# Mixing stage of a two-block kernel: another order of the work on TensorE and ScalarE, and the two best experts by plain maxima

## The reference

```python
o = o * rsqrt(mean(o * o, axis=-1) + 1e-6) * rms_w      # per head, 16 heads of 8 channels
x = x + ga * (o.reshape(B, L, Dm) @ Wout.T + bout)      # attention output, gated
h = layernorm(x) * (1 + cb) + sb                        # per token, modulated per sequence
# experts: 8, of which each token takes 2
xn     = rms_norm(h, norm_scale)
scores = einsum('bsd,ed->bse', xn, w_router)
_, ids = top_k(scores, 2)
c      = take_along_axis(softmax(scores), ids)
y      = w_down[e] @ (val * silu(gate))                 # for the two experts of each token
x      = x + gb * (sum over the two of y * c, + h)
```

## Time and profile before

| what | value |
|---|---|
| median of three runs | 2890.2 us |
| the profiled execution's own time | 2890.03 us |
| its span | 2888.2 us |
| PE, PEld, DVE busy | 2127.3, 1794.5, 1984.2 us (74, 62, 69%) |
| ACT, POOL busy | 1274.1, 1390.6 us (44, 48%) |

### The profile page before, as it was taken

The page is one execution under the profiler, slowest core; times in us unless marked ns, Lnnn a source line. Parts: engine busy times, 40 slices in busy tenths (PEclk is TensorE's granted clock), DMA queues, the critical chain, the costliest instruction groups (busy, mean ns, idle before and its releaser), DMA issues. The chain is left out here.

```text
span 2888.2 us, 43460 instructions
## 1 busy us (share of the span) xinstructions
PE 2127.3 (74%) x12482; PEld 1794.5 (62%) x12482; DVE 1984.2 (69%) x6018; ACT 1274.1 (44%) x3003; POOL 1390.6 (48%) x1241
## 2 busy tenths in 40 slices
PE   4689888888988856645466646888886655199994
PEld 4578787777878733323245535777765654199993
DVE  6677777777777879972288877787885444255556
ACT  3534444343444411212266625667773432265551
POOL 2344444544444402137355555888884244544440
PEclk8799999999999967765577778999997665599996
DMA  3000000000000030013211000000003011122216
GB/s 92 15 1 1 1 1 1 1 1 1 1 1 1 1 131 27 19 51 42 63 56 44 30 0 1 1 1 1 1 1 129 20 34 35 45 69 66 65 54 177
DMA packets 103530, 92.63 MB, mean 32 GB/s; under 512 B 11840, under 2 KB 93888, under 8 KB 102592
## 3 DMA queue, kind: packets, MB, share of 16 engines
q1 hardware_dynamic: 80256, 63.36, 7.1%
q0 software_dynamic: 14592, 22.30, 3.0%
q10 hardware_dynamic: 8448, 4.20, 0.5%
HBM read 46.84 MB, written 42.98 MB: 31 GB/s over the span
## 5 line engine op out<-in xcount | busy, mean ns | idle before, releaser
L658 PEld LDWEIGHTS attn_out<-attn_turned,attn_v_diag 128*128 128x128 f32 x2048 | 300.1, 191 | 36.1 <-issue 26.2
L658 PE MATMUL attn_out<-attn_turned,attn_v_diag 128*128 128x256 f32 (+7 forms) x2048 | 304.7, 304 | 23.6 <-DVE attn_turned L828 23.6
L716 ACT ACTIVATE attn_p_att<-attn_score,attn_mx 128x224 f32<-128x224 f32 (+7 forms) x512 | 149.1, 391 | 385.3 <-DVE attn_mx L806 385.3
L2185 POOL TENSOR_TENSOR delta_A<-delta_A,delta_sW 128x256 f32<-128x256 f32 x256 | 186.2, 727 | 98.2 <-ACT delta_sW L2065 74.2
L2002 PE MATMUL delta_u<-delta_v_own,tables_sb 128*128 128x256 f32 x512 | 161.7, 399 | 77.4 <-ACT delta_v_own L2054 77.4
L647 PE MATMUL attn_score<-attn_k,attn_q_diag 128*128 128x256 f32 (+3 forms) x1024 | 211.7, 348 | 2.3 <-ACT attn_p_att L716 2.3
L2773 POOL DMA_INDIRECT choice_rows<-ffn_y,ffn_xg x136 | 130.3, 958 | 172.5 <-DVE ffn_y L2880 168.5
L2131 DVE TENSOR_TENSOR delta_u<-delta_u,xT 128x256 f32<-128x256 f32 x256 | 153.5, 600 | 83.6 <-PE delta_u L2006 77.1
L2065 ACT ACTIVATE delta_sW<-delta_W,tables_sb 128x256 f32<-128x256 f32 x256 | 128.7, 503 | 145.6 <-issue 122.0
L2194 POOL TENSOR_TENSOR delta_m<-delta_A,qT 128x1024 f32<-128x1024 f32 x64 | 183.8, 2872 | 5.0
L704 ACT ACTIVATE attn_p_geo<-attn_kp_wide,attn_geo_cols 128x32 f32<-128x32 f32 (+6 forms) x448 | 180.1, 518 | 0.0
(11 more groups left out here) (373 smaller groups left out, 5712.4 us busy)
## 6 DMA issues: line engine op xcount, KB each, us to landing
ffn_xg<-rows SPq DMA_DIRECT2D x136, 66.0 KB
acc<-route_zero SPq DMA_DIRECT2D x10, 832.0 KB
proj_rows<-acc SPq DMA_DIRECT2D x32, 256.0 KB, 4.2
comb_rows<-choice_rows SPq DMA_DIRECT2D x32, 256.0 KB
rows<-route_rows SPq DMA_DIRECT2D x16, 320.0 KB, 3.5
load_rows<-in_x SPq DMA_DIRECT2D x16, 256.0 KB
x_kept<-xT SPq DMA_DIRECT2D x16, 256.0 KB
out<-comb_done ACTq DMA_DIRECT2D x16, 256.0 KB
```

The source lines that it names most:

```text
L658: last = nc.tensor.matmul(O[kind][:, gr * T + SLOT * n:(gr + 1) * T], v_diag[:, gr * KB + n], turned[:, kind, gr, n * T + SLOT * n:(n + 1) ...
L716: last = nc.scalar.activation(p_att[:, gr, ROW_OFF[n]:ROW_OFF[n + 1]], score[at][:, c:c + SLOT * (n + 1)], ACT.Exp, bias=mx[:, gr, n:n + 1])
L2185: nc.gpsimd.tensor_tensor(A[:, t % 8], A[:, (t - 1) % 8], sW[:, t % 4], ALU.add).then_inc(k.A, 1)
```

## The change

On TensorE the functions `project_out` and `channels` take one half and alternate, project_out first; `back(b+1)` and `sum_rows(b)` come before `router_and_rows(b)`; `sum_heads` runs one chunk further ahead and stands last. The row sums move to the PSUM bank of the head sums, with a further wait in `sum_heads` for their reading. On ScalarE `add_bias` and `modulate` alternate by halves; `copy_rows` is split, its first half ahead of `add_bias`, its second behind `square`; `exps` comes behind it and waits for the mask. On VectorE `statistics` comes before `skip`, and `choose` is written anew: for each of the two choices the largest score by a reduction, an equality with it, a product with 8 - e (`from_end`), so that among equal scores the lowest index has the largest number, its maximum, and an equality with that as the one-hot row; before the second choice the first one's score is lowered by 3e38. The exponentials are now taken of all scores in their own order, with the two best appended (10 instead of 8 columns of a tile).

```diff
-    ROUTE = 2 * SIDE + 7
-    MASKED = 2 * SIDE + 4
+    ROUTE = 17
+    MASKED = 14
+    FAR = -3.0e38
...
-        seen = s.sb("seen", [128, 2])
-        top = s.sb("top", [128, SIDE, 8])
-        top_at = s.sb("top_at", [128, SIDE, 8], U32)
+        from_end = s.sb("from_end", [128, E1])
+        best = s.sb("best", [128, SIDE, K1])
+        tied = s.sb("tied", [128, SIDE, E1])
+        first = s.sb("first", [128, SIDE])
+        rest = s.sb("rest", [128, SIDE, E1])
         onehot = s.sb("onehot", [128, SIDE, K1, E1])
         mask = s.sb("mask", [128, SIDE + 1, E1], BF16)
-        less = s.sb("less", [128, SIDE, E1])
-        ex = s.sb("ex", [128, SIDE, E1])
+        less = s.sb("less", [128, SIDE, E1 + K1])
+        ex = s.sb("ex", [128, SIDE, E1 + K1])
...
-        head_sums, narrow_ps = sums[:, 0:128], sums[:, 128:256]
-        row_sums, logits, counts = small[:, 0:SIDE], small[:, 8:8 + SIDE * E1], small[:, 72:72 + (SIDE + 1) * E1]
+        head_sums, narrow_ps, row_sums = sums[:, 0:128], sums[:, 128:256], sums[:, 256:256 + SIDE]
+        logits, counts = small[:, 0:SIDE * E1], small[:, SIDE * E1:(2 * SIDE + 1) * E1]
...
-            pe.wait_ge(c.consts, 4)
+            pe.wait_ge(c.consts, 5)
 
             def sum_heads(i):
                 if i > 0:
                     pe.wait_ge(c.heads_read, i)
+                if i > 2:
+                    pe.wait_ge(c.sums_read, i - 2)
...
-                if 0 <= b <= LAST:
-                    channels(b)
-                if b + 1 <= LAST:
-                    project_out(b + 1)
+                if b == -1:
+                    sum_heads(1)
+                for par in both:
+                    if b + 1 <= LAST:
+                        project_out(b + 1, par)
+                    if 0 <= b <= LAST:
+                        channels(b, par)
                 if b >= 1:
                     count(b - 1)
-                if b + 2 <= LAST:
-                    sum_heads(b + 2)
-                if 0 <= b <= LAST:
-                    router_and_rows(b)
                 if b + 1 <= LAST:
                     back(b + 1)
                 if 0 <= b <= LAST:
                     sum_rows(b)
+                    router_and_rows(b)
+                if b + 3 <= LAST:
+                    sum_heads(b + 3)
...
+            def copy_rows(i, par):
+                if par == 0:
+                    act.wait_ge(c.newton, ROOT * (i + 3))
+                act.wait_ge(k[par].turned, i + 1)
+                if i > 1:
+                    act.wait_ge((k[par].sent0, k[par].sent1)[i % 2], 16 * TILES * K1 * (i // 2))
+                for r in range(TILES):
+                    j = par * TILES + r
+                    last = nc.scalar.activation(rows[:, i % 2, par, r, :, 0:D],
+                                                rowt[par][:, None, 128 * r:128 * r + 128].to_broadcast([128, K1, D]),
+                                                ACT.Copy, scale=root_y[:, i % 2, j:j + 1])
+                last.then_inc(k[par].rows_read, 1)
...
-                act.wait_ge(c.route, ROUTE * i + SIDE + 1)
+                act.wait_ge(c.route, ROUTE * i + MASKED)
                 nc.scalar.activation(ex[:, :, :], less[:, :, :], ACT.Exp).then_inc(c.exp, 1)
 
             def scale_up(n):
@@ -2494,17 +2496,21 @@
                     narrow(b + 1)
                 if 0 <= b <= LAST:
                     norm(b)
-                if b + 1 <= LAST:
-                    add_bias(b + 1)
+                if b >= 1:
+                    copy_rows(b - 1, 0)
+                for par in both:
+                    if b + 1 <= LAST:
+                        add_bias(b + 1, par)
+                    if 0 <= b <= LAST:
+                        modulate(b, par)
                 if 0 <= b <= LAST:
-                    modulate(b)
                     square(b)
                 if b >= 1:
+                    copy_rows(b - 1, 1)
                     exps(b - 1)
-                    copy_rows(b - 1)
                 if 0 <= b < PIECES:
                     scale_up(b)
-                if 2 <= b + 3 <= LAST:
+                if b + 3 <= LAST:
                     head_squares(b + 3)
...
+            nc.vector.tensor_scalar(from_end[:, :], g.t("iota")[:, 0:E1], -1.0, float(E1), ALU.mult, ALU.add).then_inc(c.consts, 1)
...
-                nc.vector.tensor_copy(seen[:, 0:1], score[:, 0, 0:1])
-                for j in range(SIDE):
-                    then(nc.vector.max(top[:, j, :], score[:, j, :]), wait=False)
-                then.done()
-                if i > 0:
-                    dve.wait_ge(c.exp, i)
-                then(nc.vector.tensor_tensor(less[:, :, :], top[:, :, :], top[:, :, 0:1].to_broadcast([128, SIDE, E1]), ALU.subtract),
-                     wait=False)
-                for j in range(SIDE):
-                    then(nc.vector.max_index(top_at[:, j, :], top[:, j, :], score[:, j, :]), wait=False)
-                then.done()
-                then(nc.vector.tensor_copy(g.chosen1[:, tiles(i), :], top_at[:, :, 0:K1]))
-                then(nc.vector.tensor_tensor(onehot[:, :, :, :], g.t("iota")[:, None, None, 0:E1].to_broadcast([128, SIDE, K1, E1]),
-                                             g.chosen1[:, tiles(i), :][:, :, :, None].to_broadcast([128, SIDE, K1, E1]), ALU.is_equal))
+
+                def first_best(scores, n):
+                    then(nc.vector.tensor_reduce(best[:, :, n], scores[:, :, :], AX.X, ALU.max))
+                    then(nc.vector.tensor_tensor(tied[:, :, :], scores[:, :, :], best[:, :, n:n + 1].to_broadcast([128, SIDE, E1]),
+                                                 ALU.is_equal))
+                    then(nc.vector.tensor_tensor(tied[:, :, :], tied[:, :, :], from_end[:, None, :].to_broadcast([128, SIDE, E1]),
+                                                 ALU.mult))
+                    if n == 0:
+                        if i > 0:
+                            dve.wait_ge(c.exp, i)
+                        then(nc.vector.tensor_tensor(less[:, :, 0:E1], scores[:, :, :], best[:, :, 0:1].to_broadcast([128, SIDE, E1]),
+                                                     ALU.subtract), wait=False)
+                    then(nc.vector.tensor_reduce(first[:, :], tied[:, :, :], AX.X, ALU.max))
+                    then(nc.vector.tensor_tensor(onehot[:, :, n, :], tied[:, :, :], first[:, :, None].to_broadcast([128, SIDE, E1]),
+                                                 ALU.is_equal))
+
+                first_best(score, 0)
+                then(nc.vector.scalar_tensor_tensor(rest[:, :, :], onehot[:, :, 0, :], FAR, score[:, :, :], ALU.mult, ALU.add))
+                first_best(rest, 1)
+                then(nc.vector.tensor_tensor(less[:, :, E1:E1 + K1], best[:, :, :], best[:, :, 0:1].to_broadcast([128, SIDE, K1]),
+                                             ALU.subtract), wait=False)
                 if i > 0:
                     dve.wait_ge(c.mask, i)
                 with nc.allow_low_precision(reason="sums of one-hot rows are 0 or 1"):
-                    then(nc.vector.tensor_reduce(mask[:, 0:SIDE, :], onehot[:, :, :, :].rearrange("p j c e -> p j e c"), AX.X, ALU.add),
-                         wait=False)
+                    then(nc.vector.tensor_tensor(mask[:, 0:SIDE, :], onehot[:, :, 0, :], onehot[:, :, 1, :], ALU.add), wait=False)
...
-                then(nc.vector.tensor_reduce(total[:, :], ex[:, :, :], AX.X, ALU.add))
+                then(nc.vector.tensor_reduce(total[:, :], ex[:, :, 0:E1], AX.X, ALU.add))
                 then(nc.vector.reciprocal(total[:, :], total[:, :]))
-                then(nc.vector.tensor_tensor(g.gate1[:, tiles(i), :], ex[:, :, 0:K1], total[:, :, None].to_broadcast([128, SIDE, K1]),
+                then(nc.vector.tensor_tensor(g.gate1[:, tiles(i), :], ex[:, :, E1:E1 + K1], total[:, :, None].to_broadcast([128, SIDE, K1]),
                                              ALU.mult))
...
+                if b + 1 <= LAST:
+                    statistics(b + 1)
                 if 0 <= b <= LAST:
                     skip(b)
-                if b + 1 <= LAST:
-                    statistics(b + 1)
...
-        g.chosen1, g.gate1 = (ctx.enter_context(nc.sbuf_tensor(n, tiles, F32)) for n in ("chosen1", "gate1"))
+        g.gate1 = ctx.enter_context(nc.sbuf_tensor("gate1", tiles, F32))
```

More of the change, by code:

```diff
@@ L2324, in widen, with project_out @@
                     last.then_inc(k[par].wide, 1)
-            def project_out(i):
-                for par in both:
-                    pe.wait_ge(k[par].on, i + 1)
-                    nc.tensor.matmul(mid[par][:, :], w_out[:, :], on[:, par, :], start=True, stop=True)\
-                        .then_inc(k[par].out_made, 1)
+            def project_out(i, par):
+                pe.wait_ge(k[par].on, i + 1)
+                nc.tensor.matmul(mid[par][:, :], w_out[:, :], on[:, par, :], start=True, stop=True).then_inc(k[par].out_made, 1)
             def back(i):
@@ L2340, in back, with channels @@
```

(28 more changed lines are left out.)

34 lines of the change are left out of this document (2 added, 32 removed).

## The result

| kernel | median of 5 runs | profiled span |
|---|---|---|
| before | 2890.2 us (2885.93 to 2891.28) | 2888.2 us |
| after | 2873.25 us (2868.9 to 2875.14) | 2873.4 us |

The ratio is 0.9944, with a 95% interval of 0.993 to 0.9959. The change gains 17 us where 57 were forecast; the time lies 3 us above the range.

A forecast was written before the change was run, and what follows sets the result against it. The VectorE, TensorE, ScalarE circle was taken as the bound, GpSimd idle a third of the time. Seven steps of 126.5 + 1.5 + 42 = 170 us against 228.2, with 0.9 for the first slot: -57, so 2833 us; range 2805 to 2870.

The forecast's parts named there:

- The bound and the loop's own path: Mixing stage: VectorE, TensorE, ScalarE circle sets the pace; new loop 21.0 to 21.5 us without unexplained waits, GpSimd's floor 21.0.
- rival 1: Mixing stage becomes GpSimd-bound with no late increments: seven steps of 21.3 us, -78 us, 2812 us; chance 0.22.
- The choice: VectorE, 15 chained instructions: 3.8 us against 3.1 for the old without its stall, the extra 0.7 us hidden in steady loops.
- stall B: VectorE's unexplained 3.2 us wait behind MAX8 in each loop, read as late semaphore increments; counted as gone in steady loops.
- makes GpSimd wait in full: Choice's two-SBUF-input instructions beside indirect DMAs: would add 1.8 us a group, up to 13 us in seven steps; not expected.
- The orders: Mixing loop: statistics right behind shares, then skip, roots not waiting for row sums, first indirect DMA within 1 us of its slots.
- The unexplained waits: Late increments beside indirect DMAs in the mixing loop: 4 us a loop taken, bounds nothing to 8.2 us.
- A: VectorE's unexplained wait of about 5 us before the roots, for row sums TensorE had already finished; read as late increments.
- rival 2: Late increments stay in full in the mixing loop: 29.3 us a loop, -33 us, 2857 us; chance 0.18.
- 128.0 forecast: The first five slot steps: 25.3 us each, with 1.5 us more in the first.
- the last two: Sixth and seventh slot steps: 21.0 us each, at GpSimd's own floor, 42 us together.
- The first slot: Start of the mixing stage: first slot 0.9 us later than 2263.93, for the dearer choice.

The follow-up runs named there:

- e_after_post: Kernel after with five row buffers instead of two, GpSimd sending nothing until five chunks are routed; 2914.9 us in its only run, 20.7 us a step without DMAs.
- e_choice: The new choice alone, in the orders of the kernel before; 2877.56 us, ratio 0.9957 to the kernel before.
- e_order: The new orders alone, with the MAX8 choice of the kernel before; 2872.39 us, ratio 0.9944 to the kernel before.
- the probe: Kernel after with small stages behind its end; 64 transposes beside 16 indirect DMAs seen 10.3 us late, 0.7 with three short memsets between the DMAs.
- e_half: Kernel after with the mixing stage's squares in bf16; 2802.47 us (0.9859) beside 2843.69 before, and again 2858.97 us (0.9881) beside 2891.64.

## Why the prediction was wrong, point by point

- **The bound and the loop's own path: right.** Worked out as 21.0 to 21.5 us; 20.7 without DMAs (`e_after_post`), and 21.1 beside them on kind N, where GpSimd is the bound. On that kind rival 1 is what happens: forecast steps of 21.3, measured 21.6 in the mean.
- **The choice: right in price, without effect.** 3.5 us for 3.8, in seven of eight chunks without gaps. But the reason given for that was wrong. The prediction held that stall B needs a burst of increments as MAX8 gives; `e_choice` has gaps of 2.8 to 5.1 us a chunk in the new choice, and `e_order` has lost the wait behind MAX8 with MAX8 still there. Nor did the price matter, since the chain of choices wasn't the path: with MAX8 left in, the time was the same on kind L (2872.39 and 2873.25) and, with bf16 squares, on kind N. The prediction weighed whether, by the Trainium skill (SBUF — State Buffer, Who interferes with whom), the new choice makes GpSimd wait in full. The trace doesn't show it: of the 27 indirect DMAs that overlap the choice in the kernel after, the longest took 1.01 us, for 0.96 in the median of all 128.
- **The orders: right in what they move.** Statistics behind the shares, roots without a wait, first DMA 1.2 us behind its slots. But the score behind the roots now waits 2.5 to 7.9 us in five chunks for TensorE's router sums ("remote"), which the prediction hadn't.
- **The unexplained waits: here it failed.** The prediction said that A "sits behind TensorE's longest stretch", that the sums now come well ahead of it, and left 4 us of late increments in a loop, with 8.2 as the upper end (rival 2). The lateness isn't tied to the row sums: as the runs have it, it meets what TensorE has finished while the group of DMAs is sent, and the new orders only moved it from the row sums, which the change took off the path, to `narrow`, which is on it. There it is 12.0 us, above the 8.2 that were taken as the upper bound because they were the whole of what stood in the old loop. A step on kind L is then 1.16 us from slots to first DMA, 20.23 for the group, 2.59 until `narrow` is seen, 7.80 until the next slots: 31.8 us; with the MAX8 choice (`e_order`) such steps are 31.8 to 33.0. In the five full loops that is 158.4 us against 128.0 forecast; in the last two 49.6 against 42.
- **The first slot**: 5.4 us later instead of 0.9. 2.9 us of that were there when the stage began (its first instruction starts at 2209.8 for 2206.9), and 2.5 us came in it. But from the stage's start to the first slot the kernel after takes 56.2 us in its other profile of kind L and 55.0 on kind N, where the result's has 59.5 and the kernel before 57.0; so that part isn't the change's steady price.
- Together the miss in steps and first slot is 38.0 + 4.5 = 42.5 us: -57 becomes -14.5, and the spans differ by -14.8.
- The forecast took the chip for given. On kind N the gain is 31 us. No profile of the kernel before was taken there. If the whole gain lies in the steps, its own are (151.4 + 31.4) / 7 = 26.1 us, an estimate, and the change removes 4.5 us from each. The nearest profiles on kind N, the kernel before with bf16 squares and with the memsets, have seven steps of 171.3 and 187.4 us together, on either side of that 182.8.

What is settled: TensorE's completions are seen late, of the transfers tried only beside GpSimd's indirect DMAs, and in every run on some chips and in none on others. VectorE's gaps in the kernel go with the same chips and are gone where no DMA is under way. Open: why on some chips only, what in those DMAs does it, how it reaches VectorE, why a gap of 0.2 us takes it away in the probe (one stage, run once), and whether the gap would pay in the kernel on kind L. One rival is untested: every run here comes with a span and a granted clock, so the profiler recorded every one, and the records differ between the kinds in more than these DMAs (last section), so the recording may itself take part in the delay. The best version measured is `e_half`, 0.9881 of before on kind L and 0.9859 on kind N, with sums of squares that are rounded to bf16.

## What to carry to other kernels

When a wait ends long after the instruction that should end it, ask what else was under way and take that away from the loop: two or more such stalls that look different can have one condition in common (here the late completions of TensorE and the gaps on VectorE are both gone without the DMAs, and both on kind N), and moving work about may only choose the victim. A part whose removal and whose presence give the same time as the other part alone is a sign of a common floor; look for the floor before you price the parts. Before a gain of 1% is believed or doubted, run both kernels on a second chip.

## What the runs showed of the hardware

- The same kernel before took 2889.6 and 2891.6 us on two chips and 2843.7, 2843.0 and 2839.5 on three others. For the kernel after, the profiled spans of the result and of kind N differ by 69.1 us, 56.6 of them in the seven slot steps.
- Beside close-following indirect DMAs of GpSimd 64 TensorE transposes were seen to be done 10.1 and 10.3 us late on the former two, 0.11 us on the one of the latter where it was measured; 24 of them, or 64 beside plain DMAs, weren't late on the former (0.1 us).
- In the kernel, chained VectorE instructions beside the same DMAs have gaps on the former: 2.8 to 6.4 us a chunk in `e_choice` and `e_order`, 0.5 to 7.5 on the other chip in `e_half_again`. On the latter no choice of any kernel has one of 0.2 us.
- On the former chips the landings are missing from the record too. The DMA issues of the same kernel (line, queue, count, median us from issue to landing) give none there, but 2.3 us on the latter; so it is in all 20 profiles, 9 and 11. The same holds for 16 stores of SyncE elsewhere in the kernel (`x_kept`: none, 2.0 to 2.1 us):

```profile
rows<-mix_rows,mix_slot POOLq DMA_INDIRECT x128
```

```profile
rows<-mix_rows,mix_slot POOLq DMA_INDIRECT x128, 2.3
```
